# One shared row maximum for two key blocks in 5 of 16 query tiles of attention, and in all tiles of head 0

## What is computed

```python
Qr = jnp.einsum('bnhd,dr->bnhr', Q, WQr)
Kr = jnp.einsum('bnhd,dr->bnhr', K, WKr)
scores = jnp.einsum('bnhr,bmhr->bnhm', Qr, Kr) / math.sqrt(RANK)
A = jax.nn.softmax(scores, axis=-1)
out = jnp.einsum('bnhm,bmhv->bnhv', A, V).reshape(b, n, d)
```

## Time and profile before

| what | value |
|---|---|
| runs (3), median and ends | 2930.36 us, 2928.61 to 2930.9 us |
| the profiled execution, first to last instruction | span 2929.3 us |
| TensorE busy | 2424.4 us (83%) |
| VectorE busy | 2322.9 us (79%) |
| ScalarE busy | 1714.7 us (59%) |
| GpSimd busy | 998.7 us (34%) |
| reductions of the row scores, L745 | 2048, 1266.4 us busy, 683 ns each |
| mean granted TensorE clock | 0.923 |

### The profile page before, as it was taken

The page is one execution under the profiler, slowest core; times in us unless marked ns, Lnnn a source line. Parts: engine busy times, 40 slices in busy tenths (PEclk is TensorE's granted clock), DMA queues, the critical chain, the costliest instruction groups (busy, mean ns, idle before and its releaser), DMA issues. The chain is left out here.

```text
span 2929.3 us, 45953 instructions
## 1 busy us (share of the span) xinstructions
PE 2424.4 (83%) x14814; PEld 1063.2 (36%) x14814; DVE 2322.9 (79%) x3787; ACT 1714.7 (59%) x3510; POOL 998.7 (34%) x755
## 2 busy tenths in 40 slices
PE   8898999999999999999965988726576676688881
PEld 5322222222222222222244576602122222546761
DVE  7898999999999999999536943328799999695333
ACT  3257888888888888888815333316466465533330
POOL 3500000000000000000201477752699998036772
PEclk9879999999999999999975999957799999689996
DMA  4414111111111111111252279871343432134997
GB/s 157 129 58 135 49 49 37 37 48 49 48 37 37 48 48 48 39 35 48 87 166 97 65 214 270 203 114 20 84 112 108 111 111 82 55 107 130 286 252 200
DMA packets 255164, 293.69 MB, mean 100 GB/s; under 512 B 39120, under 2 KB 210448, under 8 KB 254928
## 3 DMA queue, kind: packets, MB, share of 16 engines
q1 hardware_dynamic: 213664, 235.09, 27.1%
q0 software_dynamic: 33104, 46.42, 8.4%
q10 hardware_dynamic: 8160, 9.32, 1.1%
HBM read 223.35 MB, written 66.75 MB: 99 GB/s over the span
## 5 line engine op out<-in xcount | busy, mean ns | idle before, releaser
L745 DVE TENSOR_REDUCE att_mx<-att_pR 128x1 f32<-128x512 f32 x2048 | 1266.4, 683 | 33.2 <-PE att_pR L785 33.1
L728 ACT ACTIVATE att_probs<-att_pS 128x512 f32<-128x512 f32 x2048 | 1063.9, 604 | 230.6 <-PE att_pS L815 230.4
L832 PE MATMUL att_pA<-att_probs,att_vh 128*17 128x512 f32 x4096 | 539.4, 598 | 12.6 <-ACT att_acc_sb L709 12.2
L815 PE MATMUL att_pS<-att_q,att_k 64*128 64x512 bf16 x1344 | 458.3, 379 | 0.3 <-ACT att_probs L728 0.2
L2177 PE MATMUL sc_pY<-sc_hc,all_ident 128*128 128x512 f32 x512 | 262.7, 638 | 125.4 <-DVE sc_hc L2134 101.2
L2043 POOL TENSOR_TENSOR sc_bh<-ssm_du,sc_b 128x1024 f32<-128x1024 f32 x128 | 297.7, 2357 | 8.9 <-issue 4.7
L672 POOL TENSOR_TENSOR att_neg<-att_mx,att_minus 128x16 f32<-128x16 f32 x32 | 7.1, 221 | 842.5 <-DVE att_mx L753 842.5
L785 PE MATMUL att_pR<-head_k,head_q 64*128 64x512 bf16 x704 | 257.6, 403 | 14.0 <-PEq L71 7.1
L815 PE MATMUL att_pS<-head_q,head_k 64*128 64x512 bf16 (+1 forms) x1408 | 263.7, 381 | 0.2
L815 PE MATMUL att_pS<-att_qs,att_ks 64*128 64x512 bf16 x1344 | 260.8, 377 | 0.2
L785 PE MATMUL att_pR<-att_k,att_q 64*128 64x512 bf16 x672 | 259.0, 385 | 0.4 <-DVE att_mx L745 0.4
(11 more groups left out here) (303 smaller groups left out, 3871.9 us busy)
## 6 DMA issues: line engine op xcount, KB each, us to landing
sc_b<-scan_rows SPq DMA_DIRECT2D x128, 256.0 KB, 3.3
expert_sum<-att_zeros SPq DMA_DIRECT2D x4, 4224.0 KB, 21.2
f1e_wgu<-in_w_gate SPq DMA_DIRECT2D x64, 192.0 KB
f1e_wgu<-in_w_up SPq DMA_DIRECT2D x64, 192.0 KB
f2e_wgu<-in_w_gate SPq DMA_DIRECT2D x64, 192.0 KB
f2e_wgu<-in_w_up SPq DMA_DIRECT2D x64, 192.0 KB
sc_c<-scan_rows SPq DMA_DIRECT2D x40, 256.0 KB, 3.4
head_q<-query_parts SPq DMA_DIRECT2D x132, 64.0 KB, 2.2
```

Source lines behind the costliest of these rows:

```text
L728: act.activation(probs[:, k % (2 * HALF), :], bank(place(k)), ACT.Exp, scale=float(DK) ** -0.5).then_inc(expd, 1)
L745: dve.tensor_reduce(mx4[s][:, k // QC, k % QC:k % QC + 1], pR[:, (s + k) % 3, :], AX.X, ALU.max).then_inc(maxed, 1)
L815: mm = pe.matmul(bank(place(k)), kk[rows, t * P:(t + 1) * P], q[rows, c * GROUP:(c + 1) * GROUP], start=not half, stop=bool(half))
L832: mm = pe.matmul(pA[32 * c:32 * c + DK + 1, :], vh[s][:, t, :], probs[:, (HALF * g + j) % (2 * HALF), :], start=(t == 0), stop=(t == KT - ...
```

## The change

For five query tiles of each head (0, 3, 6, 9 and 12), key blocks 2 and 3 share one maximum, as s3 + max(s2 - s3, 0). TensorE makes the difference s2 - s3 with two matmuls into a bank of `pS`, the second with negated keys `nk`; ScalarE takes its positive part into `diff` in SBUF; one VectorE instruction adds the row score of block 3 in `pR` and takes the largest. The row score of block 2 and its reduction go. GpSimd negates the keys once per head. Head 0 does so for all tiles and for blocks 0 and 1 too (32 folds), and head 1's first two folds are done before the loop. The fold's bank takes a place in the ring of `pS`, the left-out places go, and the place of a step now depends on the head, as 70 places are no multiple of four. The maxima of head 0 are turned after 12 row scores of head 1. The diff, cut:

```diff
-    LEFT_OUT = (16, 32, 44)
-    PLACES = STEPS + 1 + len(LEFT_OUT)
+    R_RING, DIFFS = 3, 2
+    FOLDED = (0, 3, 6, 9, 12)
+    TURN_MAXIMA = QC * FOLDED[1]
+    TURN_OF = {(QC * t - LEAD) % STEPS: t for t in FOLDED}
+    PLACES = STEPS + 1 + len(FOLDED)
...
+        def folds(n):
+            return [(t, h) for t in range(KT) for h in range(2)] if n == 0 else [(t, 1) for t in FOLDED]
+        def items(n):
+            return [k for k in range(STEPS) if (k // QC, (k % QC) // 2) not in folds(n) or k % 2]
...
         def place(k):
-            return k + sum(k >= left for left in LEFT_OUT) + (k >= SIDE)
+            return k + sum(k >= turn + 2 for turn in TURN_OF) + (k >= SIDE)
...
+        FOLD_AT = {place(turn + 1) + 1: turn for turn in TURN_OF}
...
+            for s in range(SLOTS):
+                pool.memset(mx4[s][:, :, :], NEG).then_inc(unused, 1)
...
+            def negate_keys(n, s, turn):
+                pool.wait_ge(qk_in[s], 16 * LOADS * (turn + 1))
+                for h in range(2) if n == 0 else (1,):
+                    cols = slice((2 * h + 1) * GROUP, (2 * h + 2) * GROUP)
+                    pool.tensor_tensor(nk[s][1 - h][:, :], ks[s][0:MAX_ROWS, cols],
+                                       minus[0:MAX_ROWS, 0:1].to_broadcast([MAX_ROWS, GROUP]), ALU.mult)\
+                        .then_inc(nk_ready, 1)
...
                     fetch(n + 2, (s + 2) % SLOTS)
+                    negate_keys(n + 2, (s + 2) % SLOTS, (n + 2) // SLOTS)
...
+            negate_keys(0, 0, 0)
+            negate_keys(1, 1, 0)
             fetch(0, 0)
...
+            def rise(n, t, h, scores):
+                i = folds_before(n, t, h)
+                act.wait_ge(diff_scored, i + 1)
...
+                act.activation(diff[i % DIFFS][:, :], scores, ACT.Relu).then_inc(diff_ready, 1)
...
+                        if k - 1 in TURN_OF and folded_at(n, k - 1):
+                            rise(*folded_at(n, k - 1), 1, bank(n, place(k) + 1))
...
             def maxima(n, s, steps):
                 for k in steps:
-                    dve.wait_ge(row_scored, v(STEPS * n + k + 1))
-                    dve.tensor_reduce(mx4[s][:, k // QC, k % QC:k % QC + 1], pR[:, (s + k) % 3, :],
-                                      AX.X, ALU.max).then_inc(maxed, 1)
+                    if k not in items(n):
+                        continue
...
+                    if fold in folds(n):
+                        f = folds_before(n, *fold)
+                        dve.wait_ge(diff_ready, f + 1)
+                        dve.wait_ge(row_scored, i + 1)
+                        dve.tensor_tensor_reduce(out=diff[f % DIFFS][:, :], in0=pR[:, i % R_RING, :],
+                                                 in1=diff[f % DIFFS][:, :], op0=ALU.add, op1=ALU.max, scale=1.0,
+                                                 scalar=NEG, accum_out=to).then_inc(maxed, 1)
...
+            dve.wait_ge(unused, SLOTS)
             maxima(0, 0, range(STEPS))
...
+            def fold_score(n, s, t, h, scores):
+                pe.wait_ge(nk_ready, n + 2 if n else 2)
+                rows = qs[s][0:MAX_ROWS, t * P:(t + 1) * P]
+                pe.matmul(scores, rows, ks[s][0:MAX_ROWS, 2 * h * GROUP:(2 * h + 1) * GROUP], start=True, stop=False)
+                pe.matmul(scores, rows, nk[s][1 - h][:, :], start=False, stop=True).then_inc(diff_scored, 1)
...
                         if rows:
-                            free_row(n_r, s_r, turn_r, k_r + 1)
-                            row_score(n_r, s_r, k_r + 1)
+                            row_score(n_r, s_r, turn_r, k_r + 1)
+                        if k in TURN_OF and rows:
+                            free_bank(n, place(k + 1) + 1)
+                            fold_score(n_r, s_r, TURN_OF[k], 1, bank(n, place(k + 1) + 1))
...
+            pe.wait_ge(qk_in[0], 16 * LOADS)
             for k in range(STEPS):
-                free_row(0, 0, 0, k, first=(k < 3))
-                row_score(0, 0, k)
+                if k % 2:
+                    first_fold(0, k // QC, (k % QC) // 2)
+                row_score(0, 0, 0, k)
...
             for k in range(LEAD):
-                free_row(1, 1, 0, k)
-                row_score(1, 1, k)
+                if k == TURN_MAXIMA:
+                    turn_maxima(0)
+                if (k // QC, 1) in early_folds() and k % QC == 0:
+                    first_fold(1, k // QC, 1)
+                row_score(1, 1, 0, k)
```

More of the change, by code:

```diff
@@ L514, in phase_attention @@
         mx4 = [m.sb(f"mx4{s}", [P, KT, QC]) for s in range(SLOTS)]
+        diff = [m.sb(f"diff{s}", [P, BANK]) for s in range(DIFFS)]
+        nk = [[m.sb(f"nk{s}_{h}", [MAX_ROWS, GROUP], BF16) for h in range(2 if s == 0 else 1)] for s in range(SLOTS)]
         mx = m.sb("mx", [P, KT])
@@ L525, in phase_attention @@
         inv = m.sb("inv", [P, INV])
-        pR = m.ps("pR", [P, 3, BANK])
+        pR = m.ps("pR", [P, R_RING, BANK])
         pS = m.ps("pS", [P, RING, BANK])
@@ L563, in is_head, with fold_of, items_before, folds_before @@
             return isinstance(n, int) and n == k
+        def fold_of(i):
+            n = 0
+            while i >= len(folds(n)):
+                i -= len(folds(n))
+                n += 1
+            return (n, *folds(n)[i])
         def start(n):
             return is_head(n, 0)
+        def folds(n):
+            return [(t, h) for t in range(KT) for h in range(2)] if n == 0 else [(t, 1) for t in FOLDED]
+        def items(n):
+            return [k for k in range(STEPS) if (k // QC, (k % QC) // 2) not in folds(n) or k % 2]
+        def items_before(n, k=0):
+            return sum(len(items(i)) for i in range(n)) + sum(i < k for i in items(n))
+        def folds_before(n, t=0, h=0):
+            return sum(len(folds(i)) for i in range(n)) + sum(f < (t, h) for f in folds(n))
+        def early_folds():
+            return [(t, h) for t, h in folds(1) if QC * t < LEAD]
         def place(k):
-            return k + sum(k >= left for left in LEFT_OUT) + (k >= SIDE)
+            return k + sum(k >= turn + 2 for turn in TURN_OF) + (k >= SIDE)
         SIDE_PLACE = place(SIDE) - 1
         STEP_AT = {place(k): k for k in range(STEPS)}
-        def bank(at):
-            return pS[:, at % RING, :]
-        NT = bank(SIDE_PLACE)[0:SHIFT_ROWS * KT, 0:P]
+        FOLD_AT = {place(turn + 1) + 1: turn for turn in TURN_OF}
+        assert len(set(STEP_AT) | set(FOLD_AT) | {SIDE_PLACE}) == PLACES
+        def folded_at(n, turn):
+            ahead = 1 + (turn + LEAD) // STEPS
+            return (n + ahead, TURN_OF[turn]) if n + ahead < NH else None
+        def bank(n, at):
+            return pS[:, (n * PLACES + at) % RING, :]
+        def turned_bank(n):
+            at = (n - 1) * PLACES + SIDE_PLACE if n else RING - 1
+            return pS[0:SHIFT_ROWS * KT, at % RING, 0:P]
+        def first_bank(i):
+            return pS[:, i % (RING - 1), :]
         def load_rows(eng, n, s, side, first):
@@ L772, in _, with row_score @@
         def _(pe):
-            def free_row(n, s, turn, k, first=False):
+            def row_score(n, s, turn, k):
                 if k == 0:
                     pe.wait_ge(qk_in[s], v(16 * LOADS * (turn + 1)))
-                if not first:
-                    pe.wait_ge(maxed, v(STEPS * n + k - 2))
-            def row_score(n, s, k):
+                if k not in items(n):
+                    return
+                i = items_before(n, k)
+                if i >= R_RING:
+                    pe.wait_ge(maxed, i - R_RING + 1)
                 q, kk = ((qs[s], ks[s]), (q2[s], k2[s]))[k % 2]
@@ L799, in free_bank @@
                     pe.wait_ge(expd, v(STEPS * n_before + STEP_AT[before] + 1))
+                elif folded_at(n_before, FOLD_AT[before]):
+                    pe.wait_ge(diff_ready, folds_before(*folded_at(n_before, FOLD_AT[before]), 1) + 1)
                 else:
@@ L814, in col_half @@
                 rows = slice(at, at + (MAX_ROWS, REST_ROWS)[half])
-                mm = pe.matmul(bank(place(k)), kk[rows, t * P:(t + 1) * P],
+                mm = pe.matmul(bank(n, place(k)), kk[rows, t * P:(t + 1) * P],
                                q[rows, c * GROUP:(c + 1) * GROUP], start=not half, stop=bool(half))
```

41 lines of the change are left out of this document (31 added, 10 removed).

## The result

| what | before | changed |
|---|---|---|
| median of 4 runs each | 2929.66 us | 2972.75 us (2970.73 to 2975.5) |
| ratio, 95% interval | | 1.0153 [1.0141, 1.0165] |
| profiled execution, span | 2929.3 us | 2973.6 us |
| a head of the loop, between turned maxima | 40.56 us | 41.97 us |
| first column score behind the clearing of `pA` | 49.44 us | 50.23 us |

The change makes the kernel 43 us slower. The loop has 43.7 of it (1301.9 - 1258.3), the start 0.8 (50.23 - 49.44), the other phases nothing. I predicted 2986 us from +49.5 and +6.4: the mechanism of the loop came as forecast, two terms were too big.

What follows compares the result with a forecast made beforehand. The prediction took a ring between TensorE and VectorE, 2.475 us per group, as the bound. Span 2929.3 + 49.5 (loop) + 6.4 (start) = 2985.2; with the median 1.1 above the span, 2986 us, range 2948 to 3005.

Steps and rivals of the forecast that it cites:

- the mechanism of the loop: Attention loop: fold places between a group's two pairs of steps make column scores wait for exponentials; loop sum +49.5 us.
- The ring as pace: Normal loop group: row score, its reduction, fourth row score, values, next row score set the pace, 2.475 us a group.
- Rival A: Attention loop: VectorE's load is the pace, so each fold gives back 0.47 us; 2864 us, chance 0.10.
- The bank wait: Loop fold groups: step k+3 waits for step k's exponential; 0.345 us at steps 20 and 60, 0.40 at 32, 0.225 at 48.
- The fold of step 8: Group of steps 8 to 11, with the drain: the next group's fourth row score is 0.30 us late, 9.3 us over 31 heads.
- The start: Head 0's 32 folds ahead of the loop, waiting for negated keys: +6.4 us, from +1 to +10.
- Rival B: Fused maximum on VectorE is slow, 1.22 us, and delays the next group's first row score; 3053 us, chance 0.07.
- Rival C: Loop fold groups: the bank wait is hidden and only the slot counts, 0.15 us on 92 groups; 2951 us, chance 0.12.

Runs made afterwards that it cites:

- e4: Kernel before, with each reduction of a row score reading 256 of its 512 columns: 2866.98 us, ratio 0.9792.
- e1: Kernel before, no folds, with the three left-out places of the `pS` ring moved from steps 16, 32, 44 to 22, 34, 62: 2961.71 us, ratio 1.0111.
- e5: Changed kernel, with loop folds' differences put into the freed bank of `pR` and the `pS` ring of before: 2938.77 us, ratio 1.0038.
- e7: Kernel before, with the turned maxima's place in the `pS` ring before step 52 instead of 54: 2913.38 us, ratio 0.9956.
- e6: Changed kernel without loop folds, head 0 folded, its keys negated and `mx4` filled ahead of GpSimd's other constants: 2915.06 us, ratio 0.9963.

## Why the prediction was right, and where it was off

**The ring as pace: shown as far as VectorE's load goes.** Groups without a fold stay at 2.475 us in the changed kernel, also right behind a fold, where VectorE has no work left over, and e4 bounds what relief of VectorE can bring. Rival A is refuted. The ring's parts are read from single starts; e4 shortens one of them, and the group falls until TensorE stops it. The rule of the Trainium skill that spoke for A (Perfetto Trace Analysis, Identifying the Most-Contended Engine: take the engine with the highest occupancy first) did not find the price here: after the change VectorE's occupancy fell by 37 us in 400 and the time rose; in e4, where nothing was added elsewhere, it fell by 142 and the head by 3%.

**The bank wait: shown**, by e1 without folds, by e5 with folds and no place, by e7 with the place elsewhere. Predicted 0.345 at steps 20 and 60, measured 0.345; 0.40 at 32, measured 0.405; 0.225 at 48, measured 0.23. The price read from one odd group of the kernel before held to 0.01 us at four other places.

**The fold of step 8: mis-sized.** I said that r1 of the next group is reduced 0.30 late; it was 0.07, and with it 31 x 0.23 = 7.1 us of the sum are gone. TensorE, ScalarE and VectorE of that group in the changed kernel:

```profile
648.12 0.39 PE L877 MATMUL att_pR<-head_k,head_q 64*128 64x512 bf16 x1
...
651.04 0.39 PE L877 MATMUL att_pR<-head_k,head_q 64*128 64x512 bf16 x1
...
652.28 0.39 PE L877 MATMUL att_pR<-head_k,head_q 64*128 64x512 bf16 x1
...
649.32 0.59 ACT L773 ACTIVATE att_acc_sb<-att_pA 128x512 f32<-128x512 f32 x1
...
650.27 0.62 ACT L782 ACTIVATE att_diff<-att_pS 128x512 f32<-128x512 f32 x1
...
650.92 0.69 DVE L832 CUSTOM_DVE_ANT_0 att_diff<-att_pR,att_diff 128x512 f32<-128x512 f32 x1 [1.09 <-ACT att_diff L782]
651.54 0.08 DVE L832 DVE_READ_ACCUMULATOR2_ANT att_mx<- 128x1 f32 x1
651.54 1.88 DVE L837 TENSOR_REDUCE att_mx<-att_pR 128x1 f32<-128x512 f32 x3
```

The reduction of r1 starts 3.42 behind the group's row score (651.54 - 648.12), where I had 3.64. Of these 0.22, 0.07 lie ahead of the fused maximum, which starts at 2.80 instead of 2.87 (0.05 of it, as the ReLU starts at 2.15 instead of 2.20). The other 0.15 is the failing term, the fused maximum itself: I took 0.685 + 0.08 = 0.77 as the time until the next reduction. It is 0.62 (651.54 - 650.92), since the second row and the next reduction start together, before the recorded end of the first. I had used just this for the reductions (0.69 long, 0.60 apart) and not for the new instruction. The Trainium skill (Perfetto Trace Analysis, Optimizing Scalar/DVE Operations) says that part of a recorded duration, the acknowledged write, overlaps with the next instruction; this trace agrees, with 0.69 against 0.62. The row score r4 of the next group waits for that reduction and starts 1.24 behind its group's start (652.28 - 651.04) instead of 1.17, and the group takes 2.54 instead of 2.475.

**The start: mis-sized**, +6.4 predicted, +0.8 measured. GpSimd, TensorE and VectorE at the start of the changed kernel, and its stretch table (columns as in the earlier trace rows), to be read beside the earlier trace rows:

```profile
136.11 2.03 POOL L724 TENSOR_TENSOR att_nk<-head_k,att_minus 64x512 bf16<-64x512 bf16 x2
...
138.28 0.58 PE L884 MATMUL att_pS<-head_k,head_q 64*128 64x512 bf16 x1 [22.26 <-POOL att_nk L724]
...
140.07 0.69 DVE L832 CUSTOM_DVE_ANT_0 att_diff<-att_pR,att_diff 128x512 f32<-128x512 f32 x1 [16.34 <-ACT att_diff L782]
...
163.51 0.22 DVE L844 TENSOR_REDUCE att_mx<-att_mx 128x16 f32<-128x64 f32 x1
```

```profile
140.00:145.00 5.00, 5.00 (x20) 2.12 (x19) 4.20 (x12) 3.54 (x6) 0.00 (x0) 0.53 0.00 0
145.00:150.00 5.00, 4.78 (x24) 1.43 (x21) 4.63 (x15) 4.22 (x8) 0.00 (x0) 1.00 0.00 0
```

The kernel before in the same stretch, then e6 in an earlier one:

```profile
145.00:150.00 5.00, 5.00 (x9) 0.81 (x8) 5.00 (x10) 0.00 (x0) 0.00 (x0) 0.50 0.00 0
```

```profile
130.00:135.00 5.00, 4.83 (x24) 1.49 (x21) 4.63 (x13) 4.18 (x7) 4.83 (x4) 0.93 0.26 66
```

First, a negation took 1.0, not up to 1.4: the first fused maximum came at 140.07 instead of 141.0. Second, the clock: I kept it at 0.50 (1.2 GHz), where it stands in the kernel before from 130 to 140 and still from 145 to 150. But the folds give TensorE 20 matmuls in 5 us where it had 18 in 10, and the granted clock went to 1.00 (2.4 GHz) at about 144.7, by the mean of 0.53 from 140 to 145. From there folds come 0.71 apart on average, not 0.86, and the head's maxima were done at 163.5 instead of 168.4. In e6, whose first fused maximum comes at 124.91, the clock is at 0.93 as early as 130 to 135. So its rise follows the folds; that it is the denser matmuls that raise it is read from these rows, not tried by itself. Third, the way to the first column score took 10.0 us instead of 10.6.

So both errors point the same way: I priced what the change adds at recorded durations and the old clock. The sum's span, 2985.2, stands against a profiled 2973.6, 11.6 too much: 7.1 (step 8) and 5.6 (start) too much; 1.4 us of unforeseen length in three single heads (42.61, 42.24 and 42.49) the other way. The runs' median lies lower still, as the profiled run, 2975.5 us, was the slowest of the four; its time is 1.9 above its span, not 1.1.

**Rival B** is out: 0.69 for the fused maximum, not over 0.88. **Rival C** is e5's case: its 14 us for the loop stand against 12.7 in e5's trace (1445.80 - 174.82 = 1271.0, against 1258.3).

## What to carry to other kernels

In a hand-ordered pipeline the position of a shared buffer in the order is a cost of its own, and it can be measured before any feature is written: skip the place and add nothing. A regular loop's odd group can serve as a price list (here it held to 0.01 us); read its start times, not busy shares. And an engine that is 98% busy can have its load cut by a third for 3% of the time, when its partner in the ring is as close to its own limit.

## What was not expected of the hardware

A matmul of one half of TensorE's rows starts ahead of an earlier one of the other half: in the fold group above, L916 stands behind L885 in the order of the instructions and starts at 656.72, beside L884, while L885 starts at 656.94. The trace has it so in 152 of the 155 folds of heads 1 to 31. What this is worth in time was not measured by itself. The Trainium skill (TensorEngine Tiling (Array Packing), Tiling Modes, Key Properties) says that different tiles can load and multiply in parallel; the trace agrees, and shows in addition that they need not start in order.

ScalarE's starts are 0.47 to 0.48 apart where nothing holds it (649.32, 649.79, 650.27), though each row is 0.6 long.
